# Hybrid attention, Mamba and FFN layer on one core: a new order of work where the scans begin, and a later X+U

## Chip, cores and metric

The kernel runs on one core of one Trainium2 chip. The metric is the device time of one launch in microseconds; the time before is the median of three runs.

## What is computed

The input is x of shape (16, 1024, 256) in fp32. One layer of four blocks is applied, each over a layer norm and with a residual:

```python
x = x + attention(layernorm(x), Wqkv, Wproj)          # 16 heads of 16, rotary, causal
x = x + ffn(layernorm(x), weight, bias)                # both operands rounded to a 6-bit grid in blocks of 32
x = x + mamba(layernorm(x), ...)
x = x + ffn(layernorm(x), weight, bias)
```

The Mamba block is where the change lies:

```python
xz = rmsnorm(x) @ in_proj_w.T;  xp, z = split(xz)      # 512 channels each
xc = silu(conv4(xp));  dt = softplus(...);  B, C = ...  # 16 states
h = h * exp(dt * A) + (dt * xc) * B                     # for each channel and state, along 1024 steps
y = (sum over states of h * C + xc * D) * silu(z)
x = x + y @ out_proj_w.T
x = x + silu(rmsnorm(x) @ mlp_w1.T) @ mlp_w2.T
```

## The kernel before

The loop runs over the 16 batches; everything of a batch stays in on-chip memory. Each engine has a program of its own, written out by hand, and the engines meet on semaphores, cleared at a barrier between the batches (line 1447). The order of the work on an engine is the order of its program; nothing plans it at run time. A batch goes through attention (scores on PE and row maxima on DVE, transposed scores, exponentials on ACT), the quantized product, the Mamba block, the MLP and the second quantized product. The front of the next batch's attention (layer norm, q, k and v with rotary, splitting into bf16 pieces that go through DRAM) is woven into the MLP of this one.

**The scans.** The 512 channels are 4 tiles (j) of 128 partitions, the 1024 steps are 2 halves (th), the 16 states are 8 pairs (sg). That makes 64 units n, counted with sg innermost, then j, then th. jt = n // 8 names a tile and a half. A unit takes:
- ACT: two exponentials dA, 128x512, into PSUM banks 2 and 3 (L778), each as soon as the scan before last has read its bank; then the last column of the unit before (L783); in the first tile of each half the copy of B for both states from PSUM banks 6 and 7 (L760, `spread_b`); for sg 2 and 6 of the first tile a copy of C that POOL uses later (L792).
- POOL: the product dB of dt*u with B, 128x1024 (L639), into one of two buffers; once per tile the sum that completes the next tile's dt (L635, semaphore dta); for sg 2 and 6 the product of h with C (L622), two units behind. The other units' product with C is DVE's.
- DVE: two scans of 512 steps (L1081), which need dA and dB and one of four buffers HS, which the sums of four units ago must have left (semaphore ys); then the product with C of the unit before (L1057). At sg 5 dt*u of the next tile (L1041, `times_u`), at sg 3 the gate of the tile before with silu(z) (L1064, `gate`).
- PE: it spreads B (L1312) and C (L1348) over the 128 partitions by matmuls with a selection matrix, and sums h*C over the states by matmuls with the identity into bank 4 or 5 (L1363), one pair with the diagonal of D per tile ahead of that (L1361). Step n of its loop (L1337) is: spread B for the unit after next, spread C of unit n, then the sums of unit n-1. A spread of B waits for ACT's copy of the B before; a spread of C waits for the products that read the C before.

**The way in.** Ahead of the loop over units stand: on PE the z half of the input product, tile pairs k = 0 to 7 (L1284), the last four among the first two B spreads; on ACT a softplus as Abs, Exp and Ln (L749, L753, L765), the first B copy, and z's tanh for k = 4 to 7 (L720); on DVE `times_u(0)` (L1038, L1041) and z's silu for k = 4 to 7 (L997), which multiplies tanh + 1, from the small buffer TZ, with z in PSUM. `z_bank` says which bank a z tile lies in: 2, 3, 0, 1 for k = 4 to 7. TZ lies on the first of the scans' buffers. So DVE waits for all of z's silus ahead of the first scan, ACT for two of them ahead of the first exponentials, and PE for all ahead of the scans' matmuls.

**X+U.** The MLP has 16 tile products of PE (L1388) with tanh on ACT (L803) and silu on DVE (L1106), then 8 row products (L1201). DVE writes the second half of the rows normalized for the MLP (`rms_rows(1)`, L936) behind the silu of tile 1, and the eight rows of the next front (`front_norm`, L828, semaphore fxn) behind that of tile 2. PE transposes those in pairs (L1145) between the tile products, from tile 3 on. POOL adds the Mamba block's input and output, 128x2048, in one instruction (L651, X+U, semaphore xu), as soon as the MLP's rows are written (R). SP waits for xu before it loads the next x into U; DVE waits for it at the first row product.

The lines that the steps of the prediction touch: L422 `z_bank`, L634 the dt sum's place, L651 X+U, L716 `tanh_z`, L766 the late tanhs, L778 the exponentials, L994 `silu_z`, L1337 PE's loop.

Of the kernel before, what the change touches and what calls it, by code (L numbers as in the profile page):

```python
# [8 lines left out]
ACT = mybir.ActivationFunctionType  # L9
# [83 lines left out]
def build(nc, x_in, wqkv_in, wproj_in, ipw_in, convw_in, convb_in, xpw_in, dtw_in, dtb_in, alog_in, d_in, opw_in,  # L93
          w1_in, w2_in, fw_in, fb_in, ident_in, mask_in, sel_in, cos_in, sin_in, ones_in, out):
    with ExitStack() as ctx:
# [48 lines left out]
        def view(at, n, dt=F32):  # L144
            a = arena[:, at:at + n]
            return a if dt is F32 else a.bitcast(dt)
# [47 lines left out]

        RM[1][0:NT // NTH] = [view(31248 + C * i, C) for i in range(NT // NTH)]
        SQ = view(14336, 2048).rearrange("p (i c) -> p i c", i=NT)
        TZ, TM = (view(at, 1024).rearrange("p (n t) -> p n t", n=2) for at in (28688, 13312))
        TC = view(24592, 4096).rearrange("p (j t) -> p j t", j=ND)
        DTR = view(16400, T)
        BR = view(17936, T)  # L200
# [139 lines left out]
        def S(n):  # L340
            return sem[n]
# [51 lines left out]

        POOL_SG = (2, 6)

        def b_copied(n):

            if n + 1 < NSG:
                return n + 1
            k = n - (NSG * (ND - 1) + 2)  # L400
            return NSG + k if 0 <= k < NSG else None
# [19 lines left out]

        def z_bank(k):  # L422

            return k % 4 if k < 4 else (k + 2) % 4

        def row_bank(stage, i):

# [136 lines left out]
        def pool_program(pool):  # L564
# [59 lines left out]
            for n in range(NM):  # L624
                jt, th, j, sg = m_unit(n)
                if sg == 0:
                    pool.wait_ge(S("dtu"), jt + 1)
                if j == 0:
                    pool.wait_ge(S("Be"), th * NSG + sg + 1)
                if sg == 2 and jt + 1 < NJT:  # L630

                    nth, nj = divmod(jt + 1, ND)
                    pool.wait_ge(S("dtl"), nth + 1)
                    pool.wait_ge(S("drl"), jt + 2)  # L634
                    nc.gpsimd.tensor_tensor(DT[:, nj, half(nth)], DT[:, nj, half(nth)], DTU[:, nj, half(nth)],  # L635
                                            ALU.add).then_inc(S("dta"), 1)
                if n >= 2:
                    pool.wait_ge(S("h"), SP2 * (n - 1))
                nc.gpsimd.tensor_tensor(DB[:, n % 2], DTU[:, j, half(th)].unsqueeze(1).to_broadcast([P, SP2, TH]),  # L639
                                        BB[:, SP2 * sg:SP2 * (sg + 1), :], ALU.mult).then_inc(S("dB"), 1)  # L640
                if n >= 2 and pool_c(n - 2):
                    times_kept_c(n - 2)
# [5 lines left out]
            front_power(pool)  # L648
            rms_power(1)
            pool.wait_ge(S("R"), 2 * NT)  # L650
            nc.gpsimd.tensor_tensor(X[:, :, :], X[:, :, :], U[:, :, :], ALU.add).then_inc(S("xu"), 1)  # L651
            front_pieces(pool, own, range(NT - 1))
            layer_power(2, 0)
# [24 lines left out]
        def scalar_program(act):  # L678
# [36 lines left out]

            def tanh_z(k):  # L716
                act.wait_ge(S("ip"), ND * NTH + k + 1)
                if k >= 2:
                    act.wait_ge(S("z"), k - 1)
                A(TZ[:, k % 2, :], bank(z_bank(k)), ACT.Tanh).then_inc(S("tz"), 1)  # L720

            def tanh_c(m):
                act.wait_ge(S("convd"), m + 1)
# [39 lines left out]
            for th in range(NTH):  # L763
                own.wait(own.n - NTH + 1 + th)
                A(DT[:, :, half(th)], DT[:, :, half(th)], ACT.Ln, bias=1.0).then_inc(S("dtl"), 1)  # L765
            for k in range(4, ND * NTH):  # L766
                tanh_z(k)
            for n in range(NM):
                jt, th, j, sg = m_unit(n)
                if sg == 0:  # L770
                    act.wait_ge(S("dtu"), jt + 1)
                for ss in range(SP2):
                    m = SP2 * n + ss
                    if m < SP2:
                        act.wait_ge(S("z"), 5 + m)
                    else:
                        act.wait_ge(S("h"), m - 1)
                    A(bank(da_bank(m)), DT[:, j, half(th)], ACT.Exp,  # L778
                      scale=Aneg[:, j, SP2 * sg + ss:SP2 * sg + ss + 1]).then_inc(S("dA"), 1)
                if n >= 1:  # L780
                    _, kth, kj, ksg = m_unit(n - 1)
                    if kth < NTH - 1:
                        A(hlast[:, kj, SP2 * ksg:SP2 * (ksg + 1)], HS[(n - 1) % len(HS)][:, :, TH - 1], ACT.Copy)\  # L783
                            .then_inc(S("hl"), 1)
                if b_copied(n):
                    spread_b(b_copied(n))
                if n >= 1 and kept_c(n - 1):
                    _, _, _, ksg = m_unit(n - 1)
                    act.wait_ge(S("Cg"), before(spread_c, n))
                    if before(pool_c, n - 1):  # L790
                        act.wait_ge(S("hP"), before(pool_c, n - 1))
                    A(CB[:, POOL_SG.index(ksg)], PS[:, c_bank(0):c_bank(0) + SP2, :], ACT.Copy).then_inc(S("Ce"), 1)  # L792
# [79 lines left out]
        def vector_program(dve):  # L872
# [120 lines left out]

            def silu_z(k):  # L994
                m, th = divmod(k, NTH)
                dve.wait_ge(S("tz"), k + 1)
                V_.scalar_tensor_tensor(out=Z[:, m, half(th)], in0=TZ[:, k % 2, :], scalar=1.0, in1=bank(z_bank(k)),  # L997
                                        op0=ALU.add, op1=ALU.mult).then_inc(S("z"), 1)

            for m in range(ND):  # L1000
# [41 lines left out]
                    .then_inc(S("dtu"), 1)  # L1042

            times_u(0)
            for k in range(4, ND * NTH):
                silu_z(k)
            dve.wait_ge(S("z"), ND * NTH)

            def times_c(n):

# [9 lines left out]
            def gate(jt):  # L1060

                th, j = divmod(jt, ND)
                dve.wait_ge(S("ys"), NSG * (jt + 1))
                V_.tensor_tensor(Z[:, j, half(th)], Z[:, j, half(th)], bank(4 + jt % 2), ALU.mult)\  # L1064
                    .then_inc(S("y2"), 1)

# [5 lines left out]
            for n in range(NM):  # L1072
                jt, th, j, sg = m_unit(n)
                dve.wait_ge(S("dB"), n + 1)
                if n >= len(HS):
                    dve.wait_ge(S("ys"), n - len(HS) + 1)
                for ss in range(SP2):
                    s = SP2 * sg + ss
                    m = SP2 * n + ss
                    dve.wait_ge(S("dA"), m + 1)  # L1080
                    V_.tensor_tensor_scan(HS[n % len(HS)][:, ss, :], bank(da_bank(m)), DB[:, n % 2, ss, :],  # L1081
                                          hlast[:, j, s:s + 1] if th else 0.0, ALU.mult, ALU.add)\
                        .then_inc(S("h"), 1)
                if jt + 1 < NJT and sg == 5:
                    times_u(jt + 1)
                if n >= 1 and dve_c(n - 1):
                    times_c(n - 1)
                if n >= NSG and sg == 3:
                    gate(jt - 1)
                if n - 1 in OUT_AT:  # L1090
                    add_out(OUT_AT.index(n - 1))
# [81 lines left out]
        def tensor_program(pe):  # L1173
# [144 lines left out]
            for k in range(4):  # L1318
                if k % 2 == 0:
                    spread_b(k // 2)  # L1320
                in_proj(ND * NTH + 4 + k)
            pe.wait_ge(S("z"), ND * NTH)
            pe.wait_ge(S("diag"), ND)

            def out_proj(i):
# [8 lines left out]
                    ins = MM(bank(out_bank(i))[:, 0:C], Z[:, k, tile(i)], opw[:, k, :], start=k == 0, stop=k == ND - 1)  # L1334
                ins.then_inc(S("op"), 1)

            for n in range(NM + 1):  # L1337
                if n < NM:
                    jt, th, j, sg = m_unit(n)
                    if b_copied(n + 1):  # L1340
                        spread_b(b_copied(n + 1))
                    if spread_c(n):
                        if before(dve_c, n):
                            pe.wait_ge(S("hC"), before(dve_c, n))
                        if before(kept_c, n):
                            pe.wait_ge(S("Ce"), before(kept_c, n))
                        for ss in range(SP2):
                            ins = MM(bank(c_bank(ss)), sel[:, DS + SP2 * sg + ss, :], BCP[:, half(th)],  # L1348
                                     start=True, stop=True)
                        ins.then_inc(S("Cg"), 1)  # L1350
                if n >= 1:
                    k = n - 1
                    jt, th, j, sg = m_unit(k)
                    if pool_c(k):
                        pe.wait_ge(S("hP"), before(pool_c, k + 1))
                    else:
                        pe.wait_ge(S("hC"), before(dve_c, k + 1))
                    if sg == 0 and jt >= 2:
                        pe.wait_ge(S("y2"), jt - 1)
                    if sg == 0:  # L1360
                        MM(bank(4 + jt % 2), DIAG[:, j, :], XC[:, j, half(th)], start=True, stop=False)  # L1361
                    for ss in range(SP2):
                        ins = MM(bank(4 + jt % 2), identf[:, :], HS[k % len(HS)][:, ss, :], start=False,  # L1363
                                 stop=sg == NSG - 1 and ss == SP2 - 1)
                    ins.then_inc(S("ys"), 1)
                if n in OUT_AT:
                    out_proj(OUT_AT.index(n))
# [138 lines left out]
```

## Time and profile before

| | |
|---|---|
| median of the runs shown | 9802.9 us (9801.7 to 9804.7, 3 runs) |
| the profiled execution | 9804.5 us, span 9802.8 us |
| busy: PE, DVE, POOL, ACT | 80%, 78%, 44%, 43% of the span |
| mean granted PE clock | 0.909 of full |
| DMA | 23 GB/s mean |

The rows further down count time in us from the start of the span. An engine's idle time stands in brackets, with the instruction that ended it. In a view in order of time, instructions of the same line that follow each other are merged: start, duration of the group, and their number. PE is given at 1.00 for the full clock of 2.4 GHz and 0.50 for 1.2 GHz.

### The profile page before, as it was taken

The numbers are of one execution on the slowest core, as the hardware profiler recorded it, in microseconds if no ns is written. First come the engines' busy times: TensorE is split into PE (matmuls) and PEld (weight loads), VectorE is DVE, ScalarE is ACT, GpSimd is POOL, SyncE is SP. The second block draws the span as 40 slices with busy tenths as digits, with TensorE's granted clock in tenths as the row PEclk, the third lists the DMA queues.
The fourth block names the chain that finished last, engine by engine and source line by source line (L and its number), as shares of the span: only waits on it lengthen the run. The fifth ranks groups of instructions, "written<-read, shape, count | busy, mean of one in ns | idle before, by whom it ended". The sixth has DMA issues, their size and how long they took to land. (4 is left out here: it accounts for less than half of the span.)

```text
span 9802.8 us, 98275 instructions
## 1 busy us (share of the span) xinstructions
PE 7878.8 (80%) x31796; PEld 3811.3 (39%) x31796; DVE 7618.6 (78%) x11589; ACT 4259.3 (43%) x7991; POOL 4330.9 (44%) x2631
## 2 busy tenths in 40 slices
PE   5788787887978878788887878878788787887977
PEld 2343343433434334343343434434343243432434
DVE  5787977779687696876878778787787877878777
ACT  2535435254442543525435254353534535345353
POOL 1451825418154271632726336262361724518245
PEclk8898998989989898898989889899898988989989
DMA  3020020200202002020020200102011020100202
GB/s 78 1 51 3 5 49 1 52 1 9 45 0 53 1 9 45 0 53 1 13 41 0 53 1 22 32 0 53 1 28 26 0 53 1 38 15 5 49 1 52
DMA packets 265191, 229.93 MB, mean 23 GB/s; under 512 B 26947, under 2 KB 237635, under 8 KB 264531
## 3 DMA queue, kind: packets, MB, share of 16 engines
q1 hardware_dynamic: 264678, 223.50, 10.6%
q8 instruction: 272, 4.46, 0.2%
q14 instruction: 241, 1.97, 0.1%
HBM read 151.60 MB, written 70.25 MB: 23 GB/s over the span
## 5 line engine op out<-in xcount | busy, mean ns | idle before, releaser
L639 POOL TENSOR_TENSOR arena<-arena 128x1024 f32<-128x1024 f32 x1024 | 2435.6, 2389 | 1312.4 <-DVE arena L1041 862.4
L778 ACT ACTIVATE PS<-arena,Aneg 128x512 f32<-128x512 f32 x2048 | 1410.5, 691 | 1628.1 <-DVE XNT L1081 883.6
L704 ACT ACTIVATE arena<-PS 128x512 f32<-128x512 f32 (+3 forms) x3072 | 1286.9, 508 | 861.4 <-PE PS L1249 856.9
L1363 PE MATMUL PS<-XNT,identf 128*128 128x512 f32 x2048 | 1012.2, 618 | 320.9 <-POOL XNT L622 320.9
L948 DVE TENSOR_REDUCE pm<-PS 128x1 f32<-128x512 f32 (+3 forms) x1728 | 1051.2, 663 | 271.5 <-PE PS L1228 169.6
L601 POOL TENSOR_SCALAR_AFFINE_SELECT arena<-arena 128x512 f32<-128x512 f32 x512 | 329.6, 644 | 2063.6 <-ACT arena L704 2063.6
L1225 PE MATMUL PS<-arena 96*128 96x512 bf16 (+3 forms) x3072 | 1105.5, 385 | 106.3 <-PEq L1447 49.4
L1363 PE MATMUL PS<-arena,identf 128*128 128x512 f32 x2048 | 1025.6, 625 | 161.9 <-DVE arena L1057 161.9
L1249 PE MATMUL PS<-arena 99*128 99x512 bf16 (+3 forms) x3072 | 894.5, 332 | 5.9
L1348 PE MATMUL PS<-arena,sel 96*128 96x512 bf16 x1664 | 513.7, 391 | 389.0 <-DVE arena L1057 319.5
L686 ACT ACTIVATE XNT<-PS 128x512 f32<-128x512 f32 x320 | 187.4, 597 | 1335.2 <-PE PS L1184 1334.5
L1184 PE MATMUL PS<-identf,arena 128*128 128x128 f32 x1280 | 273.4, 371 | 601.5 <-POOL arena L591 538.8
L1081 DVE TENSOR_TENSOR_SCAN arena<-PS,arena 128x512 f32<-128x512 f32 x512 | 596.9, 1207 | 129.2 <-POOL arena L639 125.6
L1261 PE MATMUL PS<-arena 128*32 128x512 f32 (+3 forms) x6144 | 651.2, 497 | 40.4 <-ACT arena L711 35.7
L1363 PEld LDWEIGHTS PS<-XNT,identf 128*128 128x128 f32 x2048 | 376.2, 193 | 739.4 <-POOL XNT L622 439.6
L1081 DVE TENSOR_TENSOR_SCAN arena<-PS,hlast,arena 128x512 f32<-128x512 f32 x512 | 627.3, 1267 | 30.8 <-POOL arena L639 21.6
L1363 PEld LDWEIGHTS PS<-arena,identf 128*128 128x128 f32 x2048 | 388.6, 197 | 669.9 <-issue 334.4
L1081 DVE TENSOR_TENSOR_SCAN XNT<-PS,hlast,arena 128x512 f32<-128x512 f32 x512 | 627.9, 1268 | 0.0
L1081 DVE TENSOR_TENSOR_SCAN XNT<-PS,arena 128x512 f32<-128x512 f32 x512 | 597.2, 1208 | 32.9 <-POOL arena L639 28.6
L622 POOL TENSOR_TENSOR XNT<-XNT,arena 128x1024 f32<-128x1024 f32 x256 | 601.8, 2351 | 47.0 <-ACT arena L792 29.0
L1057 DVE TENSOR_TENSOR arena<-arena,PS 128x1024 f32<-128x1024 f32 x512 | 614.1, 1199 | 0.0
L1225 PEld LDWEIGHTS PS<-arena 96*128 96x128 bf16 x3072 | 318.6, 104 | 700.6 <-DVE pm L948 341.6
(143 smaller groups left out, 13086.2 us busy)
## 6 DMA issues: line engine op xcount, KB each, us to landing
pieces_scratch<-arena SPq DMA_DIRECT2D x816, 64.0 KB
arena<-pieces_scratch SPq DMA_DIRECT2D x68, 384.0 KB, 10.0
arena<-pieces_scratch SPq DMA_DIRECT2D x85, 256.0 KB, 10.5
arena<-in_x SPq DMA_DIRECT2D x17, 1024.0 KB, 5.6
U<-in_x SPq DMA_DIRECT2D x17, 1024.0 KB, 5.6
arena<-pieces_scratch SPq DMA_DIRECT2D x136, 128.0 KB, 10.2
out<-X SPq DMA_DIRECT2D x64, 256.0 KB, 5.7
arena<-pieces_scratch SPq DMA_DIRECT2D x17, 768.0 KB
```

The costliest lines, as they stand in the source:

```text
L622: nc.gpsimd.tensor_tensor(hs, hs, CB[:, POOL_SG.index(ksg)], ALU.mult).then_inc(S("hP"), 1)
L639: nc.gpsimd.tensor_tensor(DB[:, n % 2], DTU[:, j, half(th)].unsqueeze(1).to_broadcast([P, SP2, TH]), BB[:, SP2 * sg:SP2 * (sg + 1), :], AL ...
L704: A(PT[s % len(PT)][:, hh, 0:w], bank(t_bank(n))[:, 0:w], ACT.Exp, scale=DH ** -0.5)\
L778: A(bank(da_bank(m)), DT[:, j, half(th)], ACT.Exp, scale=Aneg[:, j, SP2 * sg + ss:SP2 * sg + ss + 1]).then_inc(S("dA"), 1)
L948: V_.tensor_reduce(out=dst, in_=bank(r % 3)[:, 0:share * w].rearrange("p (h w) -> p h w", h=share), op=ALU.max, axis=AX.X, negate=True).th ...
L1057: V_.tensor_tensor(hs, hs, PS[:, c_bank(0):c_bank(0) + SP2, :], ALU.mult)\
L1081: V_.tensor_tensor_scan(HS[n % len(HS)][:, ss, :], bank(da_bank(m)), DB[:, n % 2, ss, :], hlast[:, j, s:s + 1] if th else 0.0, ALU.mult, A ...
L1225: ins = MM(bank(r % 3)[:, at:at + w], QS[0:SR, h, tile(i)], KS[0:SR, h, c * TH:c * TH + w], start=True, stop=not diag)
L1249: MM(bank(t_bank(n))[:, 0:w], KS[0:SR + PIECES, h, tile(j)], QS[0:SR + PIECES, h, q0:q0 + w], start=True, stop=True).then_inc(S("ST"), 1)
L1261: ins = MM(PS[VW * hh:VW * (hh + 1), 6, TH - w:TH], V[:, j, g * HG + hh, :], PT[s % len(PT)][:, hh, 0:w], start=j == 0, stop=s == last_of[oc])
L1348: ins = MM(bank(c_bank(ss)), sel[:, DS + SP2 * sg + ss, :], BCP[:, half(th)], start=True, stop=True)
L1363: ins = MM(bank(4 + jt % 2), identf[:, :], HS[k % len(HS)][:, ss, :], start=False, stop=sg == NSG - 1 and ss == SP2 - 1)
```

## The change

It does these things:
- **The last z tiles come later.** Their tanh and silu (k = 6, 7 and then 4, 5) move from ahead of the scans into the units 0 and 1, behind those units' exponentials on ACT and scans on DVE. The tanh writes to its place in Z and not to TZ, which is gone, so it no longer waits for the silu of two tiles ago. The banks of z tiles 4 to 7 become 4, 5, 0 and 1.
- **The second B copy** comes between the two exponentials of unit 0 on ACT, and no longer behind both.
- **The sums** of a unit are two steps behind on PE, in place of one. PE waits for the silu of tiles 6 and 7 ahead of the first C spread and for all silus ahead of the first sums, and no longer for all ahead of the loop; DVE no longer waits ahead of the first scan, but ahead of the first gate.
- **POOL's dt sum** for tile 1 stands ahead of dB of unit 1, before ahead of unit 2. For the other tiles it stays at sg 2.
- **X+U** also waits for the eight rows of the next front.

```diff
-        TZ, TM = (view(at, 1024).rearrange("p (n t) -> p n t", n=2) for at in (28688, 13312))
+        TM = view(13312, 1024).rearrange("p (n t) -> p n t", n=2)
...
+        Z_LATE = (6, 7), (4, 5)
+        Z_ORDER = (0, 1, 2, 3, 6, 7, 4, 5)
...
         def z_bank(k):
-            return k % 4 if k < 4 else (k + 2) % 4
+            return k if k < 6 else k - 6
...
# POOL
-                if sg == 2 and jt + 1 < NJT:
+                if sg == (2 if jt else 1) and jt + 1 < NJT:
...
             pool.wait_ge(S("R"), 2 * NT)
+            pool.wait_ge(S("fxn"), NT)
             nc.gpsimd.tensor_tensor(X[:, :, :], X[:, :, :], U[:, :, :], ALU.add).then_inc(S("xu"), 1)
...
# ACT
             def tanh_z(k):
                 act.wait_ge(S("ip"), ND * NTH + k + 1)
-                if k >= 2:
-                    act.wait_ge(S("z"), k - 1)
-                A(TZ[:, k % 2, :], bank(z_bank(k)), ACT.Tanh).then_inc(S("tz"), 1)
+                A(Z[:, k // NTH, half(k % NTH)], bank(z_bank(k)), ACT.Tanh).then_inc(S("tz"), 1)
...
-            for k in range(4, ND * NTH):
-                tanh_z(k)
             for n in range(NM):
...
-                    if m < SP2:
-                        act.wait_ge(S("z"), 5 + m)
-                    else:
+                    if m >= SP2:
                         act.wait_ge(S("h"), m - 1)
                     A(bank(da_bank(m)), DT[:, j, half(th)], ACT.Exp,
                       scale=Aneg[:, j, SP2 * sg + ss:SP2 * sg + ss + 1]).then_inc(S("dA"), 1)
+                    if m == 0:
+                        spread_b(1)
+                if n < 2:
+                    for k in Z_LATE[n]:
+                        tanh_z(k)
...
-                if b_copied(n):
+                if n and b_copied(n):
                     spread_b(b_copied(n))
...
# DVE
-                dve.wait_ge(S("tz"), k + 1)
-                V_.scalar_tensor_tensor(out=Z[:, m, half(th)], in0=TZ[:, k % 2, :], scalar=1.0, in1=bank(z_bank(k)),
+                dve.wait_ge(S("tz"), Z_ORDER.index(k) + 1)
+                V_.scalar_tensor_tensor(out=Z[:, m, half(th)], in0=Z[:, m, half(th)], scalar=1.0, in1=bank(z_bank(k)),
...
             times_u(0)
-            for k in range(4, ND * NTH):
-                silu_z(k)
-            dve.wait_ge(S("z"), ND * NTH)
...
                 dve.wait_ge(S("ys"), NSG * (jt + 1))
+                if jt == 0:
+                    dve.wait_ge(S("z"), ND * NTH)
...
+                if n < 2:
+                    for k in Z_LATE[n]:
+                        silu_z(k)
                 if n >= 1 and dve_c(n - 1):
                     times_c(n - 1)
...
# PE
-            pe.wait_ge(S("z"), ND * NTH)
             pe.wait_ge(S("diag"), ND)
...
-            for n in range(NM + 1):
+            for n in range(NM + 2):
...
                     if spread_c(n):
+                        if n == 0:
+                            pe.wait_ge(S("z"), 6)
...
-                if n >= 1:
-                    k = n - 1
+                if n >= 2:
+                    k = n - 2
                     jt, th, j, sg = m_unit(k)
+                    if k == 0:
+                        pe.wait_ge(S("z"), ND * NTH)
```

## Rows read from the trace of the kernel before

**Rows 1.** The X+U line alone: ns least, median, most; first and last start.

```profile
L651 POOL TENSOR_TENSOR X<-X,U x16: 4504/4510/4521, 625.2 to 9687.6; 128x2048 f32<-128x2048 f32 x16
```

**Rows 2.** Busy time: stretch, length, PE, PEld, DVE, ACT, POOL, PE clock, DMA share.

```profile
2231.00:2329.00 98.00, 72.57 (x187) 27.28 (x186) 95.76 (x89) 51.37 (x90) 91.77 (x42) 1.00 0.00 1
```

**Rows 3.** DVE in order of time, way in and first units of the fourth batch.

```profile
2188.78 0.69 DVE L1041 TENSOR_TENSOR arena<-arena 128x512 f32<-128x512 f32 x1
2191.77 2.70 DVE L997 SCALAR_TENSOR_TENSOR arena<-arena,PS 128x512 f32<-128x512 f32 x4 [2.29 <-ACT arena L720]
2194.50 2.34 DVE L1081 TENSOR_TENSOR_SCAN arena<-PS,arena 128x512 f32<-128x512 f32 x2
...
2198.34 2.34 DVE L1081 TENSOR_TENSOR_SCAN arena<-PS,arena 128x512 f32<-128x512 f32 x2 [1.50 <-POOL arena L639]
2200.59 1.20 DVE L1057 TENSOR_TENSOR arena<-arena,PS 128x1024 f32<-128x1024 f32 x1
...
2211.57 2.34 DVE L1081 TENSOR_TENSOR_SCAN arena<-PS,arena 128x512 f32<-128x512 f32 x2 [3.59 <-POOL arena L639]
...
2227.41 2.34 DVE L1081 TENSOR_TENSOR_SCAN arena<-PS,arena 128x512 f32<-128x512 f32 x2 [0.19 <-PE PS L1363]
```

**Rows 4.** POOL in order of time, same stretch.

```profile
2189.56 2.35 POOL L639 TENSOR_TENSOR arena<-arena 128x1024 f32<-128x1024 f32 x1 [53.90 <-DVE arena L1041]
2195.95 2.35 POOL L639 TENSOR_TENSOR arena<-arena 128x1024 f32<-128x1024 f32 x1 [4.05 <-ACT arena L760]
2198.67 1.26 POOL L635 TENSOR_TENSOR arena<-arena 128x512 f32<-128x512 f32 x1 [0.37 <-ACT arena L760]
...
2209.18 2.36 POOL L639 TENSOR_TENSOR arena<-arena 128x1024 f32<-128x1024 f32 x1 [4.32 <-ACT arena L760]
```

**Rows 5.** ACT in order of time, same stretch.

```profile
2189.84 1.28 ACT L720 ACT_TABLE_LOAD   x1
...
2193.64 1.29 ACT L778 ACTIVATE PS<-arena,Aneg 128x512 f32<-128x512 f32 x2
2194.86 1.01 ACT L760 ACTIVATE arena<-PS 128x1024 f32<-128x1024 f32 x1
```

**Rows 6.** PE in order of time, same stretch.

```profile
2201.84 1.03 PE L1348 MATMUL PS<-arena,sel 96*128 96x512 bf16 x2 [2.16 <-DVE arena L1057]
2202.67 1.91 PE L1361 MATMUL PS<-arena 128*128 128x512 f32 x2
2204.38 3.23 PE L1363 MATMUL PS<-arena,identf 128*128 128x512 f32 x4
2207.44 0.60 PE L1312 MATMUL PS<-arena,sel 96*128 96x512 bf16 x2
...
2208.31 1.88 PE L1363 MATMUL PS<-arena,identf 128*128 128x512 f32 x4
```

**Rows 7.** Busy time of one stretch, columns as in rows 2.

```profile
2196.90:2207.00 10.10, 6.41 (x11) 2.35 (x11) 8.16 (x8) 5.62 (x10) 7.33 (x4) 0.50 0.00 0
```

**Rows 8.** POOL, DVE, PE in order of time, in the MLP of the same batch.

```profile
2437.66 4.50 POOL L651 TENSOR_TENSOR X<-X,U 128x2048 f32<-128x2048 f32 x1 [1.25 <-DVE arena L936]
...
2437.49 0.68 DVE L1106 SCALAR_TENSOR_TENSOR arena<-arena,PS 128x512 f32<-128x512 f32 x1
2438.09 6.48 DVE L828 TENSOR_SCALAR arena<-arena,mv,rstd 128x256 f32<-128x256 f32 x8
...
2442.69 1.12 PE L1145 MATMUL PS<-identf,arena 128*128 128x128 f32 x4 [3.53 <-DVE arena L828]
2443.60 3.09 PE L1388 MATMUL PS<-XNT,w 128*128 128x512 f32 x4
2446.53 0.60 PE L1145 MATMUL PS<-identf,arena 128*128 128x128 f32 x4
```

**Rows 9.** The front's rows (136 in all), columns as in rows 1.

```profile
L828 DVE TENSOR_SCALAR arena<-arena,mv,rstd x136: 398/402/4237, 53.0 to 9694.1; 128x256 f32<-128x256 f32 x136
```

**Rows 10.** Busy time of one stretch in the second quantized product, columns as in rows 2.

```profile
2541.60:2545.00 3.40, 3.40 (x11) 2.78 (x10) 0.48 (x1) 0.91 (x2) 0.00 (x0) 0.50 1.09 204
```

## The prediction

> **What bounds the kernel now.** I read the busy shares first, then the period of the loop, then the two places that the diff touches, engine by engine in order of time, in the fourth of the 16 batches. X+U starts at 625.2 us in the first batch and at 9687.6 in the last [rows 1]: 15 periods of 604.16 us, so a microsecond won per batch is worth 16 us, or 0.16%. In the steady scans DVE is the bound: 95.8 us busy of 98.0, POOL next with 91.8 [rows 2]. The entry is another matter. DVE goes from the first scan (2194.50) to the ninth unit (2227.41) in 32.9 us, and it sits idle for 1.50 us ahead of unit 1 and 3.59 ahead of unit 4, both times until POOL's dB product (L639) [rows 3]. POOL had waited for an ACT copy of B (L760): 4.05 us ahead of 2195.95, 4.32 ahead of 2209.18 [rows 4]. The first copy stood behind a table load, four tanh (L720) and two exponentials: 2194.86 [rows 5]. The second stood behind PE: the sums of unit 0 (2 + 4 matmuls, 2202.67 to 2207.6) run at the half clock and the next B spread waits behind them until 2207.44 [rows 6]. The granted clock of that stretch is 0.50 [rows 7], the lower of the two levels (1.2 of 2.4 GHz), and PE had been busy for only part of it.
>
> In the MLP the chain is PE's, but it has a hole. X+U (POOL, 4.50 us) starts at 2437.66; DVE's eight rows of the next front start at 2438.09 and last 6.48 us as a group [rows 8]. Their median is 0.402 us each, the longest 4.237 [rows 9]: the first row ends only as X+U does. PE, which needs two of these rows, stands still for 3.53 us and then runs the transposes and four matmuls at the half clock (3.09 us for what takes 1.88 at the full one, [rows 6]) [rows 8].
>
> **The entry, step by step.** All times are those of the batch shown.
> (a) ACT. The table load behind the logarithms (2189.84, 1.28) must stay, now ahead of the first exponential, which starts at 2191.13 in place of 2193.64 [rows 5]. Starts follow each other by 0.6 after an exponential (1.29 for two, less one's 0.69) and 0.9 after a B copy; the four tanh lay between 2191.12 and 2193.64 with a wait of DVE's among them, so I take 0.5 each [rows 5]. So: exponential 2191.1, B copy 2191.74 to 2192.75 (was 2194.86 to 2195.87), second exponential to 2193.35, tanh 6 and 7 to 2194.36. In step 1: two exponentials, tanh 4 and 5, hlast, B copy 2 from 2196.58 to 2197.60.
> (b) POOL. dB 0 stays, 2189.56 to 2191.91 [rows 4]. The dt product's add (L635, 1.26) now comes ahead of dB 1, so dB 1 runs 2194.05 to 2196.40, 1.9 earlier than before, and no longer 3.1. dB 2 follows B copy 2: 2197.68 to 2200.03.
> (c) DVE. The four silus (2.70 [rows 3]) leave the path and return in two pairs. Scan 0 starts when dB 0 ends, at 2191.94; its second half, 1.2 long, waits for the second exponential and runs 2193.38 to 2194.60; two silus; scan 1 at 2196.43 (was 2198.34); two silus; the C product; scan 2 at 2201.0, C product to 2204.47, scan 3 at 2204.4, over at 2206.7. From scan 1 to scan 3 DVE has no idle time.
> (d) PE. Spreads of B 2, 3 and 4 and C 0 and 1 stand behind nothing but their own waits. C 2 waits for the C product of unit 1 (2204.47), and unit 0's sums now stand behind it: 2205.36, six matmuls at 0.85 each, the pace from 2202.67 to 2204.38 [rows 6], over at 2210.65. I take the half clock to the end, as PE does less up to there than before; at the full clock they would be over by 2208.9. Unit 4 reuses buffer 0 and waits for them: 2210.65, against 2211.57. So at unit 4 only 0.9 is left: the sums are what is late next.
> (e) After that the win comes back, since B 5 is spread at 2210.5 and not behind further sums (now each B copy is a step ahead of what needs it): scan 5 at 2214.6, scan 6 at 2218.6, scan 7 at 2222.0, scan 8 at 2224.46 against 2227.41. **Term A: 2.9 us**, bounds 1.0 (what unit 4 shows) and 4.9 (clock full for the sums).
> (f) Steady scans. A unit's sums must be done before the scan three units on, no longer with a unit to spare: C product, 0.06, two C matmuls (0.43, half of the time from 2207.44 to 2208.31), four sums (1.88) [rows 6] is 2.4 us. DVE needs a scan pair and a C product in the meantime, 2.34 + 1.1 = 3.4 (the product takes 1.20 and overlaps the next scan's start by 0.1) [rows 3]. Hidden, 1.0 to spare. Where a kept C leaves out the product and a diagonal product comes in (unit 36) the chain is 3.2 (two more matmuls of 0.43) against 2.9 (a scan pair and the gate's product, half as wide as a C product): 0.3 us, and POOL's wait at unit 37 and later takes most of that back. I put nothing down; bounds 0 and -0.6.
>
> **X+U behind the rows.** The eight rows then follow each other by 0.323: 2438.09 to 2440.7 in place of 2444.57. PE ends its turn at 2439.16 (2442.69 less the idle 3.53) and goes on: transposes, then h1 of tile 4 at about 2439.4 (was 2443.60), transposes, h1 of tile 5 at 2441.6; that stood at 2446.96, as the group before it, 2446.53, shows [rows 8]. **Term B: 5.3 us**, of it 4.2 for the wait and 1.2 for the half clock that follows an idle PE; bounds 3.8 (DVE's rows alone) and 5.4. X+U itself runs from 2440.7 to 2445.2. Queued behind it on POOL are the front's pieces, wanted over 10 us later, and on SP the load of U, the piece stores and the stacks, the first of which also waits for those pieces: the U load moves by some 3 us against its neighbours and is wanted in the next batch. Cost nothing.
>
> **What is given back.** From there to the quantized products everything is PE or DVE without holes, so A + B = 8.2 us arrive. There PE works on the path at clock 0.50: 11 matmuls in 3.40 us [rows 10], with the rise in the middle of the group. An advance in front of a rise that comes at its own time is worth half, because the work it wins is done at half speed. That takes 0.7 off here, and the first scores of the next batch, which start at the full clock now and would partly start at the half one, 0.6 to 0.7 more. **Term C: -1.3 us**, bounds 0 and -4.8. If several such stretches lie on the path, each halves what is left of an advance, and the loop is pulled to fixed places; the size of the give-back is therefore my weakest number, and its lower bound, more than half of A + B, comes from nothing nearer than that.
>
> **Sum:** 2.9 + 5.3 - 1.3 = 6.9 us per batch, 16 x 6.9 = 110. The profiled execution took 9804.5; minus 110 is 9694.5. The median of the runs shown is 1.6 lower: **9693**.
>
> A rule against the order of the exponentials and tanhs is in the Trainium skill, ScalarE: Activation LUTs, section "Table sets: the hidden batching unit": sets are loaded as a whole, Exp and Tanh share one, and Ln shares one with Exp. The trace agrees on the first: the exponentials behind the tanhs have no load [rows 5].
>
> **Rivals.**
> 1. *Less is given back, 9640.* Term C at 0 and A at its upper bound: 2.9 + 2.0 + 5.3 = 10.2 per batch. For it: a pull to fixed places can also go this way. Against: the sums stand at a low clock. 0.11.
> 2. *More is given back, 9748.* C at -4.8: 3.4 per batch. Same mechanism, one rise missed on the way. 0.14.
> 3. *The block moves.* X+U in its new place holds DVE's next row of the MLP (L1106) by up to 4.2 us: B is 1.2, 2.8 per batch, 9758. Against it: the L1106 row of 2437.49 took 0.68 with X+U running beside it from 2437.66 [rows 8]. 0.04.
> 4. *The table load goes elsewhere.* If the set loaded for the logarithms also held Exp, the load would come ahead of tanh 6; the B copy would be 1.3 earlier, scan 1 0.9 earlier, then the sums: 7.8 per batch, 9678. That is what the page's third statement would give. For it: nothing in the trace, where a tanh always stands behind the logarithms. 0.04.
> 5. *Slower: the sums hold the scans.* At the half clock the chain of (f) is 1.03 + 3.4 = 4.5 us [rows 6] against 3.4, 1.1 us for every unit. With sums bunched later PE may fall to the half clock in the scans more often than the one short stretch of now (the mean clock over 98 us is 1.00 [rows 2]). From 7 units in 64 on, all of 6.9 is gone; with 12 units it is 13.2 - 6.9 = 6 slower, 9900. Against: PE's work per unit stays what it was. 0.05.
> 6. *It does not do what it says.* The entry wins nothing (some B copy or dB stays last) and the rows' stall has another cause: 9803. 0.03.
> The forecast, within some 20 us, has the remaining 0.59.
>
> **Range and chances.** 9640 to 9752 takes in cases 1, 2 and 4 and leaves out 3, 5, 6 and the outer halves of 1 and 2: near 0.8. A measurement of this kernel can tell about 0.2%, 20 us, from no change. Faster by more than that: 0.92; within it 0.03; slower 0.05.
>
> **What would show it.** Right: L828's longest row near 0.4 us, PE without a gap between its turn and h1 4; a table load at L778 and none at L720; unit 0's sums behind three B spreads; the ninth unit's scan 2.9 us closer to L1041 than 38.6; a period near 597.3. Wrong: idle time on DVE ahead of scans put down to PE's L1363 in steady units (case 5); a stretched L1106 (case 3); a period near 600.7 or 593.9 (cases 2 and 1).

## The result, and the profile after

The changed kernel takes **9857.6 us** (9856.2 to 9860.3, 5 runs), against 9802.9 before: ratio 1.0056, interval 1.0041 to 1.0070. It is slower, and 165 us above the forecast. Its profiled execution took 9856.2, span 9853.6, mean granted clock 0.882 against 0.909.

X+U and the front's rows, each line alone (ns least, median, most; first and last start):

```profile
L656 POOL TENSOR_TENSOR X<-X,U x16: 4524/4531/4537, 635.2 to 9748.8; 128x2048 f32<-128x2048 f32 x16
L832 DVE TENSOR_SCALAR arena<-arena,mv,rstd x136: 404/410/415, 53.2 to 9748.2; 128x256 f32<-128x256 f32 x136
```

The period is (9748.8 - 635.2) / 15 = 607.57 us against 604.16 [rows 1], 3.41 more. But the rows' longest is 0.415 us, no longer 4.237 [rows 9]. Next come the way in and the first units of the fourth batch (the entry) on DVE, then ACT, then PE. The first line is the counterpart of L1041 in [rows 3] and stands 8.55 us later than there (2197.33 against 2188.78).

```profile
2197.33 0.69 DVE L1045 TENSOR_TENSOR arena<-arena 128x512 f32<-128x512 f32 x1
...
2205.00 2.34 DVE L1084 TENSOR_TENSOR_SCAN arena<-PS,arena 128x512 f32<-128x512 f32 x2 [0.67 <-POOL arena L643]
...
2219.29 2.34 DVE L1084 TENSOR_TENSOR_SCAN arena<-PS,arena 128x512 f32<-128x512 f32 x2 [4.04 <-PE PS L1372]
...
2233.33 2.34 DVE L1084 TENSOR_TENSOR_SCAN arena<-PS,arena 128x512 f32<-128x512 f32 x2 [0.23 <-PE PS L1372]
```

```profile
2198.39 1.28 ACT L777 ACT_TABLE_LOAD   x1
```

```profile
2213.89 1.91 PE L1370 MATMUL PS<-arena 128*128 128x512 f32 x2
2215.60 3.60 PE L1372 MATMUL PS<-arena,identf 128*128 128x512 f32 x4
```

The ninth unit's scan comes 36.00 us after that product, against 38.63: the entry did win 2.6 us. Unit 4 waits 4.04 us, now for PE's sums and no longer for POOL. In the MLP (DVE, PE, POOL) the hole of [rows 8] is gone: the tile product h1 (L1397) starts right behind the transposes and at the full clock (1.88 us where it was 3.09).

```profile
2455.07 2.67 DVE L832 TENSOR_SCALAR arena<-arena,mv,rstd 128x256 f32<-128x256 f32 x8
```

```profile
2455.97 0.60 PE L1151 MATMUL PS<-identf,arena 128*128 128x128 f32 x4
2456.41 1.88 PE L1397 MATMUL PS<-XNT,w 128*128 128x512 f32 x4
```

```profile
2457.89 4.53 POOL L656 TENSOR_TENSOR X<-X,U 128x2048 f32<-128x2048 f32 x1 [4.50 <-DVE arena L832]
```

So both aims were met. To find the loss I divided the batch at scan starts. Here are units 8 to 43 and units 44 to 63, after and before (stretch, length, PE, PEld, DVE, ACT, POOL, clock, DMA):

```profile
2233.30:2355.60 122.30, 91.82 (x233) 37.18 (x232) 118.74 (x108) 62.22 (x108) 113.16 (x51) 0.96 0.00 0
2355.60:2433.00 77.40, 60.12 (x141) 28.40 (x140) 65.97 (x62) 26.53 (x39) 57.14 (x26) 0.82 0.02 6
```

```profile
2227.40:2349.40 122.00, 91.03 (x230) 34.10 (x228) 118.63 (x108) 62.41 (x108) 113.24 (x51) 0.99 0.00 0
2349.40:2416.60 67.20, 51.11 (x140) 22.59 (x140) 65.92 (x62) 26.56 (x39) 57.23 (x26) 1.00 0.01 2
```

The last twenty units take 77.4 us in place of 67.2, with the same DVE work (65.97 and 65.92) and nearly the same count of matmuls; PE's are longer (60.12 against 51.11), and the mean granted clock is 0.82, not 1.00. That stretch holds nearly all of the loss: 10.2 us per batch. DVE's list of waits over the whole execution (us in all, times, longest) names the waiter; in the kernel before, the same entry is 72.9 us in 96 waits, the longest 1.5.

```profile
DVE U L1073 <- PE PS L1339: 219.9, 128, 3.4
```

```profile
DVE U L1070 <- PE PS L1334: 72.9, 96, 1.5
```

What waits is hardly ever a scan, but the add of an output product into U. PE around the first output product, after and then before:

```profile
2354.01 0.60 PE L1355 MATMUL PS<-arena,sel 96*128 96x512 bf16 x2
2354.44 1.88 PE L1372 MATMUL PS<-arena,identf 128*128 128x512 f32 x4
2359.24 1.03 PE L1355 MATMUL PS<-arena,sel 96*128 96x512 bf16 x2 [2.92 <-DVE XNT L1058]
2360.06 3.05 PE L1372 MATMUL PS<-XNT,identf 128*128 128x512 f32 x4
2362.95 1.89 PE L1339 MATMUL PS<-opw,arena 128*128 128x256 f32 x8
...
2407.52 1.03 PE L1355 MATMUL PS<-arena,sel 96*128 96x512 bf16 x2 [3.51 <-DVE XNT L1058]
2408.35 3.62 PE L1372 MATMUL PS<-XNT,identf 128*128 128x512 f32 x4
2411.76 2.81 PE L1339 MATMUL PS<-opw,arena 128*128 128x256 f32 x8
```

```profile
2348.45 0.60 PE L1348 MATMUL PS<-arena,sel 96*128 96x512 bf16 x2
2350.26 1.98 PE L1363 MATMUL PS<-XNT,identf 128*128 128x512 f32 x4 [1.21 <-POOL XNT L622]
2353.07 0.61 PE L1348 MATMUL PS<-arena,sel 96*128 96x512 bf16 x2 [0.82 <-DVE XNT L1057]
2353.51 1.88 PE L1363 MATMUL PS<-XNT,identf 128*128 128x512 f32 x4
2355.23 1.89 PE L1334 MATMUL PS<-opw,arena 128*128 128x256 f32 x8
```

Before, the sums of unit 42 waited for POOL's product, so PE's spare time ahead of step 44 lay in two pieces, 1.21 and 0.82 us. Two steps behind, nothing in step 43 has to be waited for; the sums follow the C spread at once, and the spare time becomes one stretch of 2.92 us. The clock is at its lower level right behind it: the C spread takes 1.03 us in place of 0.60, the sums 3.05 in place of 1.88. The output product stands behind both, and DVE gets to its add first:

```profile
2364.88 0.42 DVE L1073 TENSOR_TENSOR U<-U,PS 128x256 f32<-128x256 f32 x1 [1.61 <-PE PS L1339]
...
2380.45 0.42 DVE L1073 TENSOR_TENSOR U<-U,PS 128x256 f32<-128x256 f32 x1 [2.06 <-PE PS L1339]
...
2397.73 0.42 DVE L1073 TENSOR_TENSOR U<-U,PS 128x256 f32<-128x256 f32 x1 [2.87 <-PE PS L1339]
...
2414.61 0.42 DVE L1073 TENSOR_TENSOR U<-U,PS 128x256 f32<-128x256 f32 x1 [3.36 <-PE PS L1339]
```

And the clock of the stretch from the fourth C spread to its output product, columns as above:

```profile
2407.50:2414.40 6.90, 6.88 (x14) 3.91 (x15) 3.57 (x3) 1.38 (x2) 4.80 (x3) 0.56 0.00 0
```

PE's idle stretches ahead of these four C spreads are 2.92, 3.51, 3.55 and 3.51 us, and the waits grow from one to the next. The four are 9.9 us; before they were 0.06, 0.36, 0.06 and 0.37. A fifth wait, of 1.11 us, is one of a scan, that of unit 62, which reuses the buffer of unit 58. The view names no releaser for it, but unit 58's sums, at the half clock too, end at 2429.44, just ahead of it (PE, then DVE):

```profile
2425.82 3.62 PE L1372 MATMUL PS<-XNT,identf 128*128 128x512 f32 x4
...
2429.53 2.46 DVE L1084 TENSOR_TENSOR_SCAN XNT<-PS,hlast,arena 128x512 f32<-128x512 f32 x2 [1.11 <-issue]
```

Together that is 9.9 + 1.1 - 0.8 = 10.2, what the stretch lost.

### The profile page after: what moved, and what is told of

The parts are those of the page before. It is cut to its first block and busy times, and to the rows that moved or that the text cites. A ratio compares the mean times of both kernels' runs of the same rounds, so it can differ in the third digit from the quotient of the medians.

```text
span 9853.6 us, 98227 instructions
## 1 busy us (share of the span) xinstructions
PE 7974.6 (81%) x31796; PEld 3914.7 (40%) x31796; DVE 7560.9 (77%) x11589; ACT 4244.8 (43%) x7991; POOL 4327.8 (44%) x2631
## 5 line engine op out<-in xcount | busy, mean ns | idle before, releaser
L777 ACT ACTIVATE PS<-arena,Aneg 128x512 f32<-128x512 f32 x2048 | 1413.0, 691 | 1823.9 <-DVE XNT L1084 1062.3
L1355 PE MATMUL PS<-arena,sel 96*128 96x512 bf16 x1664 | 565.0, 425 | 918.4 <-DVE XNT L1058 569.2
L1372 PE MATMUL PS<-XNT,identf 128*128 128x512 f32 x2048 | 1144.5, 688 | 0.0
L1372 PE MATMUL PS<-arena,identf 128*128 128x512 f32 x2048 | 990.2, 606 | 0.0
L1355 PEld LDWEIGHTS PS<-arena,sel 96*128 96x128 bf16 x1664 | 123.9, 100 | 1463.2 <-DVE XNT L1058 751.5
L1372 PEld LDWEIGHTS PS<-XNT,identf 128*128 128x128 f32 x2048 | 457.4, 223 | 421.3 <-issue 356.8
```

Source lines behind the costliest of these rows:

```text
L777: A(bank(da_bank(m)), DT[:, j, half(th)], ACT.Exp, scale=Aneg[:, j, SP2 * sg + ss:SP2 * sg + ss + 1]).then_inc(S("dA"), 1)
```

## The experiments

**Theory:** the entry and the X+U wait bring what the forecast says, and the sums two steps behind take it all back by bunching PE's work: the clock falls, and the output products come late. **Rivals:** another part costs the time; or the longer chain costs it at any clock.

All stages below are of the fourth batch (of the tenth for e1, see there), in us: the start of the ninth unit's scan, counted from DVE's sum at L1038 before and L1042 after (0.73 ahead of L1041 and L1045); units 8 to 43; units 44 to 63; DVE's silu products of the MLP, called hm, from the third tile to the sixth, where the hole was; how much earlier the sixth comes than before; how much shorter the mean period is than 604.16.

| kernel | time | scan 8 | 8 to 43 | 44 to 63 | hm 2 to 5 | hm 5 earlier | period shorter |
|---|---|---|---|---|---|---|---|
| before | 9802.9 | 39.36 | 122.03 | 67.15 | 12.01 | | |
| after | 9857.6 | 36.73 | 122.28 | 77.41 | 6.64 | -3.06 | -3.41 |
| e5 two behind in tile 0 | 9693.0 | 36.75 | 121.96 | 67.15 | 6.65 | 8.06 | 6.83 |
| e1 one behind | 9696.3 | 39.15 | 122.07 | 67.14 | 6.65 | 5.55 | 6.83 |
| e2 before, two behind | 9913.5 | 37.90 | 122.85 | 75.91 | 10.39 | -6.92 | -7.05 |
| e3 before, X+U waits | 9696.0 | 39.50 | 122.08 | 67.14 | 6.64 | 5.20 | 6.83 |
| e6 filler | 9749.0 | 36.72 | 122.39 | 67.38 | 6.65 | 3.70 | 3.41 |
| e7 products at 46 | 9687.0 | 36.74 | 122.40 | 66.33 | 6.64 | 8.15 | 7.20 |
| e8 e5, no X+U wait | 9773.1 | 36.71 | 121.97 | 67.14 | 13.36 | 1.39 | 1.82 |
| e9 e5, dt sum at dB 4 | 9638.9 | 35.22 | 121.50 | 67.14 | 6.65 | 10.05 | 10.22 |
| e10 after, both moves | 9690.5 | 35.31 | 121.76 | 68.30 | 6.64 | 8.25 | 6.83 |
| e11 e9, products at 46 | 9693.8 | 35.22 | 121.54 | 70.31 | 6.65 | 6.83 | 6.82 |
| e12 e1, dt sum at dB 4 | 9692.9 | 37.48 | 121.79 | 67.14 | 6.65 | 7.50 | 6.83 |

e5, e9, e10 and e11 are medians of 4 runs, the other experiments one run each, so differences of 3 or 4 us between rows are not told from the times. The kernel before took 9799.9 to 9804.6 beside them; what an experiment won or lost against it is counted from the time beside it.

**e5, the sums two behind only up to step 8, one behind from there.**

```diff
-            for n in range(NM + 2):
+            for n in range(NM + 1):
...
-                if n >= 2:
-                    k = n - 2
+                for k in ([n - 2] if 2 <= n < 8 else [n - 2, n - 1] if n == 8 else [n - 1] if n > 8 else []):
```

> Edit: the changed kernel, with the sums two steps behind only up to unit 8 and one step behind after that. Theory (the late sums bunch PE's work in the scans, PE's clock drops to the half one there, and the output products, which stand behind it in the second half of the scans, hold DVE): DVE's waits for the output products shrink from 1.6 to 3.4 us to under 0.4 us each, the win of the entry (2.6 us at unit 8) and of the later X+U (5.4 us) stay, and the period is near 597.3 us: about 9694. Rival 1 (the lag costs by its longer chain in every tile, the first one too): unit 8 still 2.6 us ahead, so no different here. Rival 2 (the late z tiles or the later X+U cost the time): still above 9803.

Measured: 9693.0 (9690.4 to 9693.7), ratio 0.9887, interval 0.9871 to 0.9904. The entry is that of the changed kernel, the late scans those of the kernel before:

```profile
2323.30:2390.50 67.20, 51.10 (x140) 22.58 (x140) 65.92 (x63) 26.53 (x39) 57.22 (x26) 1.00 0.01 3
```

So 164.6 us of the changed kernel's time hang on the sums behind step 8 alone.

**e1, the changed kernel with the sums one behind throughout.**

```diff
-            for n in range(NM + 2):
+            for n in range(NM + 1):
...
-                if n >= 2:
-                    k = n - 2
+                if n >= 1:
+                    k = n - 1
```

> Edit: the changed kernel with the sums one step behind throughout, as before the change. Theory: no half-clock stretches between units 45 and 63, no waits for the output products; the entry wins less, since unit 0's sums stand ahead of the B spread again (unit 8 under 1 us ahead of before, not 2.6); period 597.3 to 600.8, 9694 to 9750. Rival 2 (z tiles or X+U cost the time): above 9803.

Measured 9696.3. The ninth unit's scan is 2.4 us later than in e5 and only 0.2 earlier than in the kernel before: with the sums one behind, the rest of the new entry wins next to nothing. Yet the period is e5's, to 0.01 us. The fourth batch is the odd one here: unit 0's four sums took 2.23 us in it and 3.62 in the tenth, and its ninth scan came at 38.19, where the other fifteen batches have 39.04 to 39.16. One and the same program can so lie a microsecond apart from batch to batch, and a single batch is not enough to rank versions by.

**e2, the kernel before with the sums two behind** and nothing else: the diff of e1 the other way round, in the kernel before.

> Edit: the kernel before, with the sums two steps behind and nothing else. Theory: the half-clock stretches in units 45 to 63 and the waits for the output products appear here too, some 10 us per batch, less what the entry wins by B spreads that no longer stand behind sums (1 to 2 us); period above 610, over 9880. Rival 2 (other parts of the change cost the time): within 20 us of 9803 or faster.

Measured 9913.5: this edit alone costs 109 us, and DVE's waits for the output products are 200.6 us in all, against 72.9. It is the cause, and needs no other part of the change. (One of its periods is 614.3 us, the rest are 611.0.)

**e3, the kernel before with the X+U wait** and nothing else.

```diff
             pool.wait_ge(S("R"), 2 * NT)
+            pool.wait_ge(S("fxn"), NT)
```

> Edit: the kernel before, with X+U behind the front's rows and nothing else. Theory: tile 5's silu in the MLP 5.4 us earlier after the last scan than before, part of it given back at the half clock later; period 600.8 or 597.3, 9750 or 9694. Rival 2 in the form that X+U costs more than it wins: above 9803.

Measured 9696.0: 109 us from one wait. The stretch from hm 2 to hm 5 went from 12.01 to 6.64.

**e6, clock or chain?** The changed kernel with matmuls of no use in the long idle stretches: it keeps the sums two behind and gives PE more to do.

```diff
+                if n >= 39 and n < NM and m_unit(n)[3] in (3, 7):
...
+                    for r in range(4):
+                        MM(bank(7 if n < 48 or 52 <= n < 56 else 6), identf[:, :], XC[:, 0, half(0)], start=True, stop=True)
```

> The changed kernel with four 512-column float32 matmuls of no use (1.88 us at full clock) at the end of every seventh PE step, the one before each long idle stretch of PE (steps 39, 43, ... 63), sums still two steps behind. Theory (late sums bunch PE's work, the clock falls in the idle stretch, and the output products at half clock are late): the idle stretches shrink from 2.9 to 3.6 us to about 1.7, the clock stays full in units 44 to 63, DVE's waits of 1.6 to 3.4 us before the output adds fall under 0.5, scan 63 starts some 227 to 229 us after the first times-U instead of 236.4, and the time is 9693 to 9750. Rival (the chain of sums and output product is simply too long two steps behind, at any clock): the waits stay at 1.6 or more and the time is 9857 or more, since PE only got more work.

Measured 9749.0, 108.7 us less than the changed kernel. Each of the four calls is two matmuls in the trace, so a group is 8 in 3.60 us and not the 1.88 that I wrote:

```profile
2335.27 3.60 PE L1383 MATMUL PS<-arena,identf 128*128 128x512 f32 x8
2338.70 0.60 PE L1355 MATMUL PS<-arena,sel 96*128 96x512 bf16 x2
2339.14 1.88 PE L1372 MATMUL PS<-XNT,identf 128*128 128x512 f32 x4
2340.86 1.89 PE L1339 MATMUL PS<-opw,arena 128*128 128x256 f32 x8
```

```profile
2334.80:2402.20 67.40, 65.72 (x181) 30.86 (x180) 65.88 (x62) 26.55 (x39) 57.26 (x26) 1.00 0.01 2
```

```profile
DVE U L1073 <- PE PS L1339: 77.7, 112, 1.5
```

PE is busy for 65.72 of 67.40 us, the clock is back at 1.00, the C spread at 0.60 and the sums at 1.88, and the four waits are down to 0.31, 0.36, 0.06 and 0.35. The longer chain is not the cause: with 40 more matmuls in the stretch it is in time. Most of what keeps e6 from e5's 9693 is its last filler group, in step 63, with real work of PE queued behind it: from scan 63 to hm 2 it takes 24.6 us, e5 20.9 and the changed kernel, with the same sums and no filler, 21.45.

**e7, the output products after steps 46, 50, 54 and 58**, away from the idle stretch.

```diff
-        OUT_AT = [44 + 4 * i for i in range(NT // NTH)]
+        OUT_AT = [46 + 4 * i for i in range(NT // NTH)]
```

> The changed kernel with the four output products of the first half two steps later (after steps 46, 50, 54, 58 instead of 44, 48, 52, 56), so that they no longer stand right behind PE's long idle stretch. Theory (what costs is only that the products run late and slow behind that stretch): DVE's waits before the output adds fall from 1.6 to 3.4 us to under 0.5 each, scan 63 starts 227 to 230 us after the first times-U, time 9693 to 9750, even if some stretches at half clock remain. Rival (the scans themselves wait for the late sums, through the buffers of H): other waits take their place, and the time stays at 9857 or more; in between, 9800, if the clock's fall slows the C spreads as well.

Measured 9687.0, 6 us below the range that I gave. They are of the start: its first two periods are 594.4 and 594.7 us, and from the third on it has e5's 597.33. PE still idles and slows ahead of step 44:

```profile
2324.39 1.04 PE L1355 MATMUL PS<-arena,sel 96*128 96x512 bf16 x2 [2.90 <-DVE XNT L1058]
2325.22 3.08 PE L1372 MATMUL PS<-XNT,identf 128*128 128x512 f32 x4
...
2332.35 1.89 PE L1339 MATMUL PS<-opw,arena 128*128 128x256 f32 x8
```

```profile
2320.80:2387.10 66.30, 50.63 (x141) 23.79 (x140) 65.70 (x62) 26.48 (x39) 57.23 (x26) 0.97 0.01 2
```

The waits for the output products are 0.29 us at most: nobody waits for what is slow there. So the changed kernel's loss needs both: the low clock, and a product behind it that DVE wants at once.

**e8, e5 without the X+U wait:** the entry alone.

```diff
-            pool.wait_ge(S("fxn"), NT)
```

> The kernel of sums two steps behind in the first tile only, without the wait of X+U for the MLP's rows: the new entry alone, against the kernel before. The entry brings 2.6 us per batch at the scans' end. If the periods of the batches move only in whole steps of about 3.4 us, the time is 9803 (nothing), 9748 (one step) or 9693 (two), and 9760 if wins are passed on as they are. The stretch from h 2 to h 5 in the MLP is 12 us as in the kernel before, not 6.6.

Measured 9773.1, none of the values that I named. The periods alternate, 600.9 and 604.0 us, so the entry alone brings 1.8 us per batch on average; the sixth tile comes 1.4 us earlier than before in one batch, as in the fourth, and 3.0 in the next. The hole in the MLP is there (13.36).

**e9, e5 with POOL's dt sum for tile 1 ahead of dB 4** and not dB 1.

```diff
-                if j == 0:
-                    pool.wait_ge(S("Be"), th * NSG + sg + 1)
-                if sg == (2 if jt else 1) and jt + 1 < NJT:
+                if sg == (2 if jt else 4) and jt + 1 < NJT:
...
                                             ALU.add).then_inc(S("dta"), 1)
+                if j == 0:
+                    pool.wait_ge(S("Be"), th * NSG + sg + 1)
```

> The kernel of sums two steps behind in the first tile only, with POOL's sum of dt rows for tile 1 (1.27 us) moved from ahead of the product dB 1 to ahead of dB 4. Scan 1 starts 0.9 to 1.3 us closer to the first times-U than 8.40, scans 2 and 3 some 1 us closer, and the end of the scans at most 1 us closer. If wins are passed on as they are: 9680. If the period moves only in whole steps of about 3.4 us: 9693 (nothing) or 9640 (one step).

Measured 9638.9 (9636.1 to 9640.3), ratio 0.9832, interval 0.9816 to 0.9849: the best version found, 163 us faster than the kernel before beside it. DVE has no idle time ahead of scan 1, and scan 8 comes 1.5 us earlier than in e5:

```profile
2165.17 2.33 DVE L1084 TENSOR_TENSOR_SCAN arena<-PS,arena 128x512 f32<-128x512 f32 x2
2167.42 1.26 DVE L1001 SCALAR_TENSOR_TENSOR arena<-arena,PS 128x512 f32<-128x512 f32 x2
```

Scan 1 came only 0.76 closer, less than the 0.9 to 1.3 expected, since DVE's own silus are last there now; scan 8 came 0.5 closer than I allowed.

**e10 and e11, both moves:** the diffs of e7 and e9 together, in the changed kernel with its sums two behind throughout (e10) and in e5 (e11).

> The changed kernel, sums two steps behind throughout, with both moves that the last runs bear out: the output products after steps 46, 50, 54 and 58, and POOL's dt sum for tile 1 ahead of dB 4. Both together should give the scans' end some 2 us per batch ahead of the version with the output products alone moved (9687): 9634 to 9640 if the period again moves by 3.4 us, 9655 if wins are passed on as they are. If the half-clock stretches of the scans in units 10 to 48 cost more beside the earlier entry: 9660 to 9690.

> The version with sums two steps behind in the first tile only and the dt sum ahead of dB 4 (9639), with the output products two steps later as well. The adds waited 0, 0.36, 0 and 0.37 us in the first half with sums one behind, so the move has at most 0.7 us per batch to win: 9628 to 9639, and 9639 if the period only moves in steps of 3.4 us.

Measured 9690.5 (e10) and 9693.8 (e11). e11 is a plain miss, 55 us slower than e9. With sums one behind, unit 45's sums wait for DVE's product, and the output product of step 46 stands right behind them (PE, then DVE's add):

```profile
2334.29 1.98 PE L1371 MATMUL PS<-arena,identf 128*128 128x512 f32 x4 [1.15 <-DVE arena L1058]
2336.11 1.89 PE L1339 MATMUL PS<-opw,arena 128*128 128x256 f32 x8
```

```profile
2338.03 0.42 DVE L1073 TENSOR_TENSOR U<-U,PS 128x256 f32<-128x256 f32 x1 [1.43 <-PE PS L1339]
```

The four waits are 1.43, 0.85, 1.44 and 0.85 us, and units 44 to 63 take 70.31 us against 67.14. PE is at the full clock in the rows shown, so this loss needs no low clock: the place in the queue is enough. I had looked only at what the adds waited for, not at what the product would stand behind. In e10 the same units take 68.30, at a mean clock below one again (0.95); it ends half a microsecond above the range that I gave for that case.

**e12, e1 with the diff of e9:** are two steps needed in the entry?

> Sums one step behind throughout, as in the kernel before, with all the rest of the change and POOL's dt sum ahead of dB 4: does the entry need the sums two behind at all? One behind, the eighth unit's scan stood at 38.2 us after the first times-U, against 36.75 with two behind in the first tile; the earlier dB 1 should take some 1 us off, to 37.0 to 37.4, against 35.2 for the version with two behind (9639). If the period moves in steps of about 3.4 us, the 1.4 us between them is either nothing (9639) or a whole step (9693); if wins are passed on as they are, 9660.

Measured 9692.9: yes. Its sixth tile comes 2.55 us later than e9's, and the time is 54 us longer. (The 38.2 from which I expected its ninth scan was that of e1's odd batch. From the 39.15 of the others the earlier dB 1 took 1.7 off.)

## Why the prediction was wrong

- **(a) to (e), the entry: right.** Less the offset of 8.55, unit 0's sums start at 2205.34 (2205.36 forecast), unit 4 at 2210.74 (2210.65), unit 8 at 2224.78 (2224.46). Term A is 2.6 us and not 2.9. By e1 nearly all of it hangs on the later sums: with the sums one behind it is 0.2.
- **Term B: right.** 12.01 - 6.64 = 5.37 us, forecast 5.3; e3 shows it alone. The Trainium skill, SBUF — State Buffer, section "Who interferes with whom", has a rule that fits: GpSimd (POOL) and VectorE (DVE) share a port pair, and against a VectorE instruction in a two-port mode, which `tensor_scalar` can take, whoever issues first has the pair for the whole instruction while the other blocks. The trace agrees: X+U started first (2437.66, the rows at 2438.09), one row of L828 took 4.237 us beside X+U's 4.50, and 0.415 is the longest now. No run here shows in which mode the rows run.
- **Term C: the size came out, by luck; the mechanism did not.** In e5, which has A and B without the fault, 8.06 us arrive at the sixth tile and 6.83 are left, so 1.23 are given back (1.3 forecast), and the time is the forecast's 9693. But e3's 5.20 and e1's 5.55 become 6.83 as well, and e12's 7.50 too. Nothing is halved there: in these runs an advance is rounded, up or down.
- **(f), the steady scans: the step that failed.** It says "Hidden, 1.0 to spare", "I put nothing down; bounds 0 and -0.6". At the full clock the chain to the next scan was right; one scan of units 44 to 63 waits, 1.1 us, behind sums at the half clock. Two things were left out. PE's later consumers: the output product of steps 44 to 56 stands behind the sums, and DVE adds it a unit later. And the clock: I took 1.88 us for four sums from a row at the full one, without asking what moving them does to PE's idle time. The term, put at nothing, measured 10.2 us per batch; 2.6 + 5.4 - 10.2 = -2.2. Units 8 to 43 lose 0.25 more and the way from scan 63 to hm 2 0.55 (21.45 against 20.90), which makes the -3.06 at the sixth tile.
- **Rival 5 had the mechanism's first half**, with a chance of 0.05: sums bunched later, PE at the half clock in the scans. The second half was wrong: it had scans wait for sums, 12 units at 1.1 us, 9900. It was four output products, 1.6 to 3.4 us each, and 9857.6. My argument against it, that PE's work per unit stays what it was, is no argument: the work did stay (141 matmuls against 140), its spacing did not. e6 tests this: with the idle stretches filled the clock stays at 1.00 and the waits go.
- **Rivals 1 to 4 and 6.** The DVE products at L1112 took 0.69 with X+U beside them, so 3 did not happen. The table load is at L777 and none stands ahead of the late tanhs, so 4 fell. The Trainium skill, ScalarE: Activation LUTs, section "Table sets: the hidden batching unit", says that Ln and then Exp need one load, since one set holds both. In this program's trace it is not so: a load of 1.28 us stands between the two. Rival 1's 9640 was reached, but by e9's further edit. Rival 2's 3.4 us per batch is what e6 kept, not this kernel. Both wins are there, so 6 fell.

## What to carry to other kernels

Before moving work on PE, write down its idle pieces before and after, not only its busy sum: two waits of 1.2 and 0.8 us that became one of 2.9 cost more here than the waits that were removed. Follow everything queued behind the moved work in every kind of iteration, the rare ones too (here 4 of 64 units). A rescheduling that is right for the entry of a loop can be confined to the entry: e5 and the changed kernel differ in nothing else, and by 165 us.

## What the hardware showed that I had not expected

**Useless work made the kernel faster.** e6 has 14.6 us more PE work in units 44 to 63 (65.72 against 51.11 before) and is 108.7 us faster than the changed kernel, which has none. It is still 56 us slower than e5, which has no late sums to mend. The Trainium skill, TensorE: Matmul & The Clock Gate, section "HAM oscillation — how this bites in real kernels", tells of idle pauses between bursts of matmuls after which each next burst starts throttled. The trace agrees that a burst behind a pause runs slow (2.92 us idle, then a C spread of 1.03 us for 0.60).

**The period took few values.** Thirteen kernels have periods of 593.94 (e9), 597.33 (e1, e3, e5, e10, e11, e12, and e7 from its third on), 600.75 (e6), 604.16, 607.57 and 611.0 us (e2, but for one of 614.3); e8 goes back and forth between two. e1, e3 and e5 reach the sixth tile 5.5, 5.2 and 8.1 us earlier than before, and end within 0.01 us of each other in the period. So a gain of 2 us was worth nothing in one pair of versions and 3.4 us per batch in another (e12 against e1, e9 against e5), and parts don't add up: the entry alone brought 29 us, X+U alone 109, both together 112. That the clock's rises hold the loop to such places was only argued; no run here tests it, and the cause stays open.
